# Two full-width products whose result nobody reads, in front of each group of the narrow modulation products

## What is computed

```python
# block 0, on x; c is (2, 256)
ada = silu(c @ ada1_w + ada1_b) @ ada2_w + ada2_b        # (2, 1536)
shift_msa, scale_msa, gate_msa, shift_mlp, scale_mlp, gate_mlp = split(ada, 6, axis=1)
x = x + gate_msa * modulate(layernorm(attention(x, mask)), shift_msa, scale_msa)   # 16 heads of 16
x = x + gate_mlp * modulate(layernorm(gelu(x @ fc1_w + fc1_b) @ fc2_w + fc2_b), shift_mlp, scale_mlp)
# block 1
emb = silu(t) @ ada_w + ada_b                            # (2, 1536), t is the same c
x = x + gate_msa * (gelu((ln(x) * (1 + scale_msa) + shift_msa) @ ssm_w1 + ssm_b1) @ ssm_w2 + ssm_b2)
x = x + gate_mlp * (gelu((ln(x) * (1 + scale_mlp) + shift_mlp) @ ff_w1 + ff_b1) @ ff_w2 + ff_b2)
```

## Time and profile before

| | us |
|---|---|
| median of three runs (389.63 to 392.27) | 389.87 |
| the profiled execution | 392.98 |
| its span, first to last instruction | 391.3 |
| TensorE busy in the span | 355.3 |
| VectorE busy | 250.6 |
| ScalarE busy | 231.7 |
| GpSimd busy | 177.3 |

### The profile page before, as it was taken

One profiled execution on the slowest core, in us unless ns is written; L12 is line 12 of the kernel. 1 busy time (PEld: TensorE's weight loads), 2 busy tenths in 40 slices (PEclk: granted clock), 3 DMA queues, 4 the chain that ended last, 5 costly groups with the idle time before them and its releaser, 6 DMA issues. The chain is left out here.

```text
span 391.3 us, 7654 instructions
## 1 busy us (share of the span) xinstructions
PE 355.3 (91%) x2606; PEld 288.3 (74%) x2606; DVE 250.6 (64%) x565; ACT 231.7 (59%) x440; POOL 177.3 (45%) x185
## 2 busy tenths in 40 slices
PE   6699599999999999999999999999989999976681
PEld 5587496455699967697897849699965989965671
DVE  5566727689972499988838795834556655454521
ACT  5523134678456588976787789796558656432530
POOL 1537169203526633261354543636653654653440
PEclk9789655799999999999999999999999999997797
DMA  7598943536442031401101010000000000000001
GB/s 242 188 345 292 303 152 141 167 115 203 128 166 100 2 86 39 105 0 58 43 1 43 3 42 3 27 3 28 3 0 2 1 29 29 0 0 2 0 30 34
DMA packets 20182, 30.90 MB, mean 79 GB/s; under 512 B 1933, under 2 KB 12807, under 8 KB 20136
## 3 DMA queue, kind: packets, MB, share of 16 engines
q1 hardware_dynamic: 16664, 23.24, 19.3%
q10 hardware_dynamic: 3472, 7.08, 5.4%
HBM read 21.20 MB, written 8.80 MB: 77 GB/s over the span
## 5 line engine op out<-in xcount | busy, mean ns | idle before, releaser
L601 POOL TENSOR_TENSOR p_hid<-p_gelu,p_hid 128x512 fp32r<-128x512 f32 x56 | 73.2, 1310 | 70.6 <-ACT p_hid L771 70.3
L876 DVE TENSOR_REDUCE p_nmax<-ps 128x2 f32<-128x512 f32 x128 | 82.4, 682 | 23.4 <-PE ps L1127 20.5
L740 ACT ACTIVATE p_probs<-ps 128x512 f32<-128x512 f32 x128 | 68.5, 602 | 18.3 <-PE ps L1139 16.5
L619 POOL TENSOR_TENSOR x_all<-x_all,p_vec 128x512 f32<-128x512 f32 x32 | 41.1, 1290 | 47.7 <-DMA p_vec<-pmod_dram 23.7
L1005 PE MATMUL ps<-p_fc_hi,p_hid 128*128 128x256 f32 x256 | 52.7, 289 | 0.8 <-POOL p_hid L601 0.8
L762 ACT ACTIVATE p_gelu<-ps,p_column 128x256 f32<-128x256 f32 x64 | 26.8, 469 | 28.8 <-PE ps L1005 27.6
L1005 PEld LDWEIGHTS ps<-p_fc_hi,p_hid 128*128 128x128 f32 x256 | 41.5, 188 | 3.2 <-POOL p_hid L601 1.2
L1005 PE MATMUL ps<-p_m_hi,p_fc_hi 128*128 128x256 f32 x128 | 36.8, 287 | 0.0
L762 ACT ACTIVATE p_gelu<-ps,p_upb_mod 128x256 f32<-128x256 f32 x48 | 20.1, 471 | 27.9 <-PE ps L1005 27.7
L771 ACT ACTIVATE p_hid<-p_gelu 128x512 fp32r<-128x512 f32 x56 | 35.2, 632 | 2.0 <-PE ps L1005 0.5
L1005 PE MATMUL ps<-p_fc_lo,p_hid 128*128 128x256 f32 x128 | 36.0, 281 | 0.0
(11 more groups left out here) (196 smaller groups left out, 881.8 us busy)
## 6 DMA issues: line engine op xcount, KB each, us to landing
p_qa<-pq_dram SPq DMA_DIRECT2D x28, 192.0 KB, 3.7
pq_dram<-p_qk_buf SPq DMA_DIRECT2D x6, 512.0 KB, 3.1
p_vec<-pmod_dram SPq DMA_DIRECT2D x4, 512.0 KB, 3.9
out<-x_all SPq DMA_DIRECT2D x8, 256.0 KB, 2.2
p_probs<-in_L_cond_ada_w ACTq DMA_DIRECT2D x1, 1536.0 KB, 9.3
pq_dram<-p_qk_buf SPq DMA_DIRECT2D x6, 256.0 KB, 4.5
p_adb_raw<-in_L_cond_ada_w ACTq DMA_DIRECT2D x1, 1536.0 KB, 9.8
x_all<-in_x SPq DMA_DIRECT2D x3, 512.0 KB, 5.7
```

The lines of the kernel that those rows point to most:

```text
L601: pool.tensor_tensor(hid[:, TOOK[of][0], 1, :], gelu_out[:, TOOK[("gelu",) + step[1:]][0], :], hid[:, TOOK[of][0], 0, :].bitcast(F32), ALU ...
L619: pool.tensor_tensor(tiles(m, h), tiles(m, h), vec[:, m // NCH, SHIFT[L], :].rearrange("p (o c) -> p o c", o=1).broadcast_to([P, 2, C]), A ...
L740: act.activation(probs[:, kt, 2 * p + e, :], ps[:, TOOK["s2", a, g, kt, p][e], :], ACT.Exp, scale=SCALE).then_inc(s_exp, 1)
L876: dve.tensor_reduce(nmax[:, u % 2, e, 0, at:at + 2], ps[:, TOOK["s1", a, g, j][e], :].rearrange("p (t n) -> p t n", t=2), axis=AX.X, op=AL ...
```

## The change

A helper issues two products of 256 columns each: stationary operand the first 128 columns of the high weights of the queries, moving operand the first 256 columns of the same rows. They write columns 256 to 511 of the bank that the narrow products write in their first 24 (or 12) columns; nothing reads what they write. The helper is called once ahead of each block's two narrow products, in `ada` and in `upb`. The first step of each `ada` waits for the queries' low weights in addition. `ada1` has no such products.

```diff
@@ -1012,6 +1012,11 @@
+        def keep_clock(bank):
+
+            for _ in range(2):
+                pe.matmul(bank[:, HALF:CH], weights["qkv"][0][:, 0, 0:P], weights["qkv"][0][:, 0, 0:C], start=True, stop=True)
+
@@ -1077,11 +1082,13 @@
                 if i == 0:
+                    pe.wait_ge(*wlo_done("q"))
                     pe.wait_ge(s_silu, 3)
                     pe.wait_ge(s_ada_raw[n], 16)
                     take(step)
                 dst = ps[:, TOOK["ada", n, 0][0], :]
                 for f in range(i * 6 * KC // ADA_PARTS, (i + 1) * 6 * KC // ADA_PARTS):
+                    keep_clock(dst)
                     for k in range(KC):
```

## The result

| | before | changed |
|---|---|---|
| median, us (runs) | 391.07 (4) | 396.36 (4) |
| lowest to highest, us | 389.63 to 392.57 | 393.97 to 397.27 |
| ratio, 95% interval | | 1.0133 (1.0085 to 1.0182) |
| profiled execution, us | 392.98 | 397.04 |
| its span, us | 391.3 | 395.3 |

The change costs 1.3%, 5.3 us by the medians; the forecast was +6.6 us and 396.5.

The account below looks back on a forecast made before the run. TensorE, busy 355.3 of 391.3 us, was taken as the bound. 0.35 + 5.3 + 1.8 = 7.5 us, less 0.9 taken up, gave +6.6: 396.5 on the median of 389.87; range for 8 in 10, 383.5 to 399.0.

Parts of the forecast that it names:

- rival B: Half clock through ada/1, but full again by upb/0, 8.6 us further on before: +2.3 us, 392.2; chance 15%.
- wrong altogether: Signs against the forecast: clock of 1.00 from s1/0/2/0, or that step starting 2 us later, the pause being no cover.
- Half clock through ada/1: Clock stays at 0.50 from before s1/0/2/0 to behind q/2/0 despite the wide products.
- 24 wide products in ada/1 cost 5.3 us: In ada/1, 24 x 0.22 us at half clock, all on the path since TensorE has no pause up to 72.8.
- Rival C: One of two wide products is free in ada/1 and upb: half the price, +3.1 to 3.5 us, 393.2; chance 10%.
- Part 2: 24 wide products in ada/1: 5.3 us, with half of it as lower bound if a weight load is hidden.
- Part 1: Wide products in ada/0: the 4.41 us pause ahead of s1/0/2/0 covers them; its end moves 0 to 0.7, taken as 0.35.
- Part 3: Twelve wide products in upb, four at half clock and eight at full: 1.8 us, 2.6 if all at half.
- Part 4: The added wait for the queries' low weights, already met earlier, and the shared bank: both cost nothing.
- What the pauses and the tail take up: TensorE's 4.6 us of pauses up to 346 us and the tail take up 0.9 us of the sum.
- Rival A: Full clock holds from the pause at 42 us through ada/1: -6.1 us, 383.8; chance 15%.
- the idle gap: Skill's rule at the pause: 1.6 us shorter could keep the clock up; the trace's fall at 42 us disagrees.

Follow-up runs that it names:

- block 1 alone: Wide products in the four ada/1 steps only (24 of 60), against the kernel before: ratio 1.0092 (1.0048 to 1.0136), +3.6 us.
- Four a group: The changed kernel with four wide products ahead of each group in place of two (120 in all): ratio 1.0263, +10.3 us on the kernel before.
- four and 16: The changed kernel with four wide products per group and 16 in the pause ahead of s1/0/2/0: ratio 1.0083 (0.9997 to 1.0169) to the kernel before.
- four in the shadow: Kernel before plus four wide products per group in the last two ada/0 steps and ada/1, 14 ahead of s1/0/2/0, none elsewhere: ratio 0.9978, median 388.69 us.
- two-column run: The changed kernel's 60 unread products with 2 columns in place of 256: ratio 1.0129 (1.0086 to 1.0172) to the kernel before.
- upb alone: Wide products in the three upb steps only (12 of 60), against the kernel before: ratio 1.0037 (0.9997 to 1.0077), +1.4 us.
- the pause alone: Kernel before with 20 unread wide products ahead of the waits of s1/0/2/0, none among the narrow ones: ratio 0.9935 (0.9885 to 0.9984), -2.5 us.
- block 0 alone: Wide products in the four ada/0 steps only (24 of 60), against the kernel before: ratio 0.9989 (0.9925 to 1.0054).
- the filled pause: The changed kernel with 20 more unread wide products ahead of the waits of s1/0/2/0: ratio 1.0024 (0.9980 to 1.0069) to before, median 391.94 us.

## Why the prediction was right, and which of its steps were not

The sign, the range and nearly the size came out: +5.3 us against +6.6. That 396.36 lies so near to 396.5 is luck to a part, since the kernel before has a median of 391.07 here and had 389.87 in the forecast. And two errors of opposite sign helped: s1/0/2/0 started 3.85 us later where the sum has 0.35, and q/2/0 to upb gave 2.6 us back where the sum adds 1.8. By the prediction's own signs the half clock through ada/1 and the longer groups (0.44 us; measured 0.42) were right; the full clock at upb/0 (72.4 us) is its sign of rival B, and s1/0/2/0 more than 2 us late is one that it called wrong altogether. The work behind 110 us was to be shifted by 6 to 7 us; at the last transpose of the attention it is 5.0 (305.47 against 300.51).

- **Half clock through ada/1: right.** 50.4 to 68.8 at 0.50, in the changed kernel twice with the pause open, and with block 1 alone, where there was no pause. So two a group didn't bring the clock back even in 30.6 us without a stop (39.0 to 69.6). Four a group didn't either, from 49.6 to 83.6 in their one profile with the pause open; with the pause filled and the clock full ahead of it they held it (four and 16, and four in the shadow).
- **24 wide products in ada/1 cost 5.3 us: right in size, the reason left open.** Measured +5.13 in that stretch. The prediction took the pace of other wide products, 0.22 us, as nearest row, without saying what in them takes the time. The two-column run shows that it isn't the columns: the price is the same for 2 and for 256.
- **Rival C (one of two is free): wrong.** The first step of ada/1 grew from 2.65 to 3.92 us (51.11 to 55.03), which is 0.42 us a group and the price of both (2 x 0.21). The 256 columns add nothing to it, so they do run beside the loads, but all six loads of a group follow each other and nothing is saved. Part 2's lower bound of half the price didn't come out. The Trainium skill, "TensorE: Matmul & The Clock Gate", section "Part 2: What happens when you issue a matmul", says that the next load is pulled ahead of a running product; the 1.28 us with 2 columns and with 256 agree with that, and in them the loads themselves stand in line.
- **Part 1, the pause as cover: sized wrong.** The term was 0 to 0.7 us. The wait ahead of s1/0/2/0 ended at 46.0 to 47.5 in three profiles without wide products in block 0 (before, upb alone, the pause alone) and at 48.0 to 50.4 in five with them in all its steps, 2.6 us later on average. In the others the pause was filled or TensorE was late, so that the start doesn't tell. ScalarE shows the way. Two of its steps wait for stores to free their buffer; before:

```profile
30.29 0.60 ACT L694 ACTIVATE p_qk_buf<-ps 128x512 fp32r<-128x512 f32 x1 [3.27 <-DMA pq_dram<-p_qk_buf]
...
35.92 1.23 ACT L645 ACTIVATE p_qk_buf<-ps,p_one_rows,p_low_sign 128x512 fp32r<-128x512 f32 x2 [4.58 <-DMA pq_dram<-p_qk_buf]
```

and in the changed kernel:

```profile
33.29 0.60 ACT L694 ACTIVATE p_qk_buf<-ps 128x512 fp32r<-128x512 f32 x1 [5.52 <-DMA pq_dram<-p_qk_buf]
...
40.06 1.24 ACT L645 ACTIVATE p_qk_buf<-ps,p_one_rows,p_low_sign 128x512 fp32r<-128x512 f32 x2 [5.71 <-DMA pq_dram<-p_qk_buf]
```

These waits ended 3.0 and 4.1 us later. SyncE sends for the packed keys (L485) behind the store of what the first of the two steps writes, at 35.58 before and at 38.55 in the changed kernel, and s1/0/2/0 starts 11.0 and 11.8 us behind that. TensorE itself was not late at the start of this: ada/0/0 begins at 23.53 and 23.57. But that the wide products delay this chain isn't shown. Counted from ada/0/0, the keys are sent for after 12.1 to 13.3 us or after 14.5 to 15.2. Of seven profiles with wide products in the first two ada/0 steps four have the late time (the changed kernel twice, block 0 alone, two columns) and three don't (the filled pause, both with four everywhere); of the seven without, one has it (four in the shadow). What decides between the two is open, and the time of block 0 alone didn't rise.
- **Rival B (the clock is back earlier): it came about, beside the forecast.** q/2/0 ran at half clock for 2.5, 3.8 and 4.0 us in the three profiles of the first point, and for 12 to 13 us in the four without wide products in ada/1 (before, block 0 alone, upb alone, the pause alone). In the changed kernel that gave back about 4 us of q/2/0 to upb: 2.6 in the table, and the price of upb's own 12 products. It isn't the columns of the added products that do it, since in the two-column run the clock was back 3.0 us into q/2/0 too (and fell again at 72.9). Of the two other profiles with two a group in ada/1 and half clock at q/2/0, both with a filled pause, it was back after 3.6 and 4.1 us; with four a group and an open pause it took 11.7 us. So the early return goes with the added products in six profiles of seven and is seen in none of the four without. The prediction's argument against B, that such luck comes to both kernels, was the step that failed. Why the clock returns there was not settled.
- **Part 3, upb +1.8: +1.4 (-0.1 to +3.0) alone.** In the changed kernel upb/0 ran at full clock, so its price there was less: 12 x 0.115 = 1.4.
- **Part 4, the added wait: nothing, as said.** The pause alone has the wait as well and is no slower than before.
- **What the pauses and the tail take up, 0.9:** 1.40 and 0.96 in the profiles, 2.4 in place of 0.9; the tail alone differs by up to 3.7 us between profiles without the edit's doing.
- **Rival A (the level holds): not in the changed kernel.** It decided where the prediction said, at the pause: half clock at s1/0/2/0. But the filled pause shows that the level can be raised there, and that two a group don't hold it through ada/1.
- **On the idle gap.** The Trainium skill, "TensorE: Matmul & The Clock Gate", in "Why this matters for your kernels", names gaps between bursts as what brings the clock down. The prediction weighed this lightly, as the clock had fallen ahead of the pause. With the gap filled and the narrow products left alone the clock came back at 45.2 and 2.5 us were gained by the ratio, which fits the rule. The falls at 42.1 before, at 54.1 in the changed kernel with the filled pause and at 52.0 in the pause alone, each in a TensorE that had not stopped for 4.5 us and more, don't fit it.

## What to carry to other kernels

Put unread products that are to keep the clock up where the engine would stand still anyway: 20 of them in a pause gained 0.65% (0.2 to 1.2), 60 of them among the working products lost 1.3%. Price such a product by what one more product in the chain costs, not by its columns (up to the 256 measured here), and count that the dose that holds the clock (four to each pair here) may cost what the clock gives. A kernel whose executions differ by 12 us from one to the next needs a dozen of them before a change of 1% can be read, and one profile of it doesn't tell where half a per cent lies.

## What was unexpected

- A product with 2 columns and one with 256 took the same time in a chain of products that each load new weights: 1.28 us a group both ways at half clock.
- The kernel before, 35 executions in one set: 385.57 to 397.77 us. The mean granted clock was 0.946 and 0.947 in the two below 386 us, and 0.923 in the highest.
- With the clock at 1.00 from 22 to 352 us the kernel was no faster than one with 30.7 us of half clock in that time, since 136 unread products took what it gave.
